# Copies of a block's masked factors issued from ScalarE's queue instead of SyncE's

## What is computed

```
xn = layernorm(x); sx = shifted(xn) - xn
x5 = xn + sx * (maa_stack + lora(xn, sx))              # five mixes: k, w, v, r, g
w  = exp(-exp(time_decay + lora(x5.w)))
r, k, v, g = x5.r @ Wr.T, x5.k @ Wk.T, x5.v @ Wv.T, silu(x5.g @ Wg.T)
for t in tokens:                                       # 32 heads of 16
    out[t] = r[t] @ (u * outer(k[t], v[t]) + s)
    s      = outer(k[t], v[t]) + w[t][:, None] * s
x = x + (groupnorm(out) * g) @ Wo.T
x = x + sigmoid(xr @ ffn_Wr.T) * (relu(xk @ ffn_Wk.T) ** 2 @ ffn_Wv.T)   # on layernorm(x)
```

## Time and profile before

| | us |
|---|---|
| median of 3 runs | 1509.73 |
| lowest and highest run | 1508.66, 1511.53 |
| the profiled execution, its own time | 1514.45 |
| span of the profiled execution, first to last instruction | 1512.7 |

### The profile page before, as it was taken

How to read it: one execution, slowest core, us unless ns; L and a number is a source line. 1 busy time by engine, 2 the same in 40 slices (tenths; PEclk the granted TensorE clock), 3 DMA queues, 4 the chain that set the end, 5 groups by cost and what they waited for, 6 DMA issues and landing times.

```text
span 1512.7 us, 52040 instructions
## 1 busy us (share of the span) xinstructions
PE 1443.9 (95%) x22980; PEld 1074.9 (71%) x22980; DVE 910.2 (60%) x1990; ACT 517.4 (34%) x910; POOL 599.2 (40%) x528
## 2 busy tenths in 40 slices
PE   8988999999999999999999999999999999999888
PEld 7867776757778676876767778576776757777464
DVE  3667557565676656657574676657657565665542
ACT  1323423424333333423433332333423424332332
POOL 3343515225262432615235262443615226262421
PEclk9999999999999999999999999999999999999899
DMA  8011102011010111102011110111102011010110
GB/s 309 6 42 49 42 12 69 18 40 54 28 55 15 41 54 37 55 12 70 18 41 54 28 55 14 41 55 38 55 19 63 18 40 54 14 55 15 56 33 28
DMA packets 56449, 68.13 MB, mean 45 GB/s; under 512 B 23264, under 2 KB 40032, under 8 KB 55200
## 3 DMA queue, kind: packets, MB, share of 16 engines
q1 hardware_dynamic: 56224, 64.79, 13.9%
HBM read 43.75 MB, written 8.39 MB: 34 GB/s over the span
## 4 chain that ended last, share of the span: by engine, by line
PE 84%; DVE 8%; SPq 3%; issue 2%; ACT 1%; DMA 1%; POOL 1%; DVEq 0%; ACTq 0%; POOLq 0%
PE pairs L1223 32%; PE pairs L1242 20%; PE at_ps L1151 4%; PE pairs L1234 4%; PE at_ps L1144 3%; SPq L406 3%; DVE x L778 3%; PE pairs L1250 3%; PE pairs L1266 3%; PE att_ps L1214 2%; PE pairs L1287 2%; PE pairs L1332 1%; PE pairs L1305 1%; PE pairs L1311 1%; PE pairs L1299 1%
## 5 line engine op out<-in xcount | busy, mean ns | idle before, releaser
L1223 PE MATMUL pairs<-x,wts 128*128 128x256 f32 x1760 | 397.0, 380 | 1.0 <-DVE lag L802 0.5
L1223 PEld LDWEIGHTS pairs<-x,wts 128*128 128x128 f32 x1760 | 328.4, 190 | 51.1 <-issue 7.0
L974 ACT ACTIVATE at<-at_ps 128x512 f32<-128x512 f32 x128 | 76.4, 597 | 386.1 <-PE at_ps L1151 193.5
L548 POOL TENSOR_TENSOR x<-x,xnT 128x1024 f32<-128x1024 f32 (+1 forms) x79 | 158.4, 2005 | 65.3 <-DVE x L778 65.3
L778 DVE SCALAR_TENSOR_TENSOR x<-pairs,vecs,sx 128x256 f32<-128x256 f32 x316 | 129.0, 474 | 87.0 <-PE pairs L1266 76.9
L558 POOL TENSOR_TENSOR bonv<-bonv,lag 128x256 f32<-128x256 f32 x32 | 27.1, 848 | 226.7 <-DVE lag L798 226.7
L1151 PE MATMUL at_ps<-rm,kc 128*16 128x128 f32 (+1 forms) x2048 | 112.8, 278 | 3.3 <-issue 3.3
L1223 PE MATMUL pairs<-yT,wts 128*128 128x256 f32 x512 | 113.8, 380 | 1.3 <-DVE gT L809 1.3
L1242 PE MATMUL pairs<-wts,cen 128*128 128x512 f32 x240 | 108.9, 606 | 4.5 <-DVE x L778 4.5
L1242 PE MATMUL pairs<-wts,yT 128*128 128x512 f32 x240 | 107.1, 599 | 1.6 <-POOL yT L585 1.6
L1223 PEld LDWEIGHTS pairs<-yT,wts 128*128 128x128 f32 x512 | 95.9, 190 | 14.2 <-DVE gT L809 1.5
(11 more groups left out here) (197 smaller groups left out, 2626.1 us busy)
## 6 DMA issues: line engine op xcount, KB each, us to landing
rm<-rst SPq DMA_DIRECT2D x1024, 12.0 KB
xu<-in_x SPq DMA_DIRECT2D x16, 512.0 KB, 3.9
wts<-in_wts SPq DMA_DIRECT2D x8, 1024.0 KB, 14.5
kvs<-in_s SPq DMA_DIRECT2D x32, 256.0 KB, 2.9
s<-in_s SPq DMA_DIRECT2D x32, 256.0 KB, 3.9
x<-in_x SPq DMA_DIRECT2D x15, 512.0 KB, 5.1
out<-sx SPq DMA_DIRECT2D x15, 512.0 KB, 3.0
prev<-in_prev SPq DMA_DIRECT2D x32, 4.0 KB, 3.8
```

The source lines that it names most:

```text
L548: gp.tensor_tensor(t, t, old, ALU.add).then_inc(x5_ready, 1)
L974: ac.activation(at[:, :, :], at_ps[:, :].rearrange("p (h t) -> p h t", h=HG), ACT.Copy)\
L1223: last = pe.matmul(ps[:, g // 2, TB * (g % 2):TB * (g % 2 + 1)], wts[:, m, k, g * P:(g + 1) * P], source[:, k, :], start=(k == 0), stop=(k ...
```

## The change

The copies of units 2 to 7 leave SP's list. `mask` on SP serves only units 0 and 1. On ACT, `evict` issues, directly behind its copy of unit n's products, the eight DMAs of unit n+2 within the same sequence; behind unit 3's copy it issues those of units 4 and 5, and behind those of units 2, 6 and 7 none. A new function `load_mask` does it; it waits for `rchain`, and the wait on `levels_done` is the one that `evict` has made already.

```diff
-SP_ORDER = ["x", "S0", "M1", "F1", "M2", "M3", "out", "x2", "S1", "M4", "M5", "F0", "M6", "M7", "M0"]
+SP_ORDER = ["x", "S0", "M1", "F1", "out", "x2", "S1", "F0", "M0"]
...
-    0: ["M1", "x", "F1", "M2", "M3", "out", "x2", "S1", "M4", "M5", "F0", "M6", "M7", "M0"],
-    LAST: ["S0", "M1", "F1", "x2@0", "x2@1", "M2", "M3", "M4", "out", "x2", "S1", "M5", "M6", "M7"],
+    0: ["M1", "x", "F1", "out", "x2", "S1", "F0", "M0"],
+    LAST: ["S0", "M1", "F1", "x2@0", "x2@1", "out", "x2", "S1"],
...
-                    elif name[0] == "M" and name != "M0" and units(i):
+                    elif name == "M1" and units(i):
                         mask(at_, int(name[1:]))
...
                 ac.activation(at[:, :, :], at_ps[:, :].rearrange("p (h t) -> p h t", h=HG), ACT.Copy)\
                   .then_inc(at_ready, 1)
+                for unit in {G - 2: (), G - 1: (G, G + 1), UNITS - 2: (), UNITS - 1: ()}.get(n, (n + 2,)):
+                    load_mask(at_, unit)
+
+            def load_mask(blk, n):
+
+                b, g, p = n // G, n % G, n % 2
+                ac.wait_ge(rchain, blk.count(2 * NR, NR * (b + 1)))
+                for h in range(HG):
+                    ac.dma_start(rm[p][S * h:S * (h + 1), h, :], rst[S * h:S * (h + 1), b, g, R16C:R64A])\
+                      .then_inc(rm_in[p], 16)
```

## The result

| | before | after |
|---|---|---|
| median, us | 1510.63 | 1783.67 |
| lowest and highest, us | 1508.66, 1513.22 | 1782.87, 1785.94 |
| ratio to before | | 1.181, interval 1.179 to 1.184 |
| span of the profiled execution, us | 1512.7 | 1782.2 |
| mean granted clock of PE | 0.991 | 0.914 |

The change costs 273 us; the prediction was 1778 us in 1685 to 1830. DVE's and POOL's lines are as before.

The account below looks back on a forecast made before the run. PE, busy 95% of the span, was taken to bound the kernel. Fifteen blocks at 14.2 us of stalls plus 3.4 of clock give 264, - 5 for the first blocks, + 10 for the last: 269, median 1778 us, range 1685 to 1830.

Parts of the forecast that it names:

- Price of a batch: ACT's list: eight copy issues hold it 5.65 us, sixteen 11.3, the same as on SP.
- Units 4 and 5, at kv1 and k.0: Behind E3, sixteen issues delay kt1 and z's tanh, so PE stalls at kv1 and k.0: 9.3 us.
- Unit 3, at hs_1: Behind E1, eight issues delay vtm1, so PE's hs_1 starts late: 4.9 us a middle block.
- Unit 2, at gn_sum: Behind E0, DVE's gn_sum starts 1.65 us late; 0.5 us is left over, inside the next stall: cost 0.
- a sign of being wrong: Prediction's test: wrong if a stall turns up at a place costed at nothing, such as gn_sum or r.
- Units 6 and 7: Behind E4 and E5: r's copy moves later, but g.0 needs its bank 3.4 us later still: cost 0.
- Clock: PE's clock falls once for each of two stalls, 1.7 us each, 3.4 us a block.
- yT: Last block, behind E3: sixteen issues make yT 10.3 us late, POOL's gate and wo follow: + 10.
- the clock holds: Rival: PE's clock doesn't fall, only the stalls cost, 15 x 14.2 = 213, + 5: 1728 us; chance 0.16.
- Queues hinder each other: Rival: ACT and SP take turns issuing, unit 2's batch takes 10 to 11 us: 1793 to 1838 us; chance 0.07.
- ACT issues as fast as the shortest row on SP: Rival: ACT's batch of eight takes 2.6 us, stalls of 5.1 us a block: 1605 us; chance 0.06.
- issues on ACT cost next to nothing: Rival: both stalls vanish below about 0.1 us an issue, leaving earlier copies: 1503 us, faster; chance 0.09.

Follow-up runs that it names:

- unit 2 alone: Against the kernel before, only unit 2's eight copies moved to ACT, behind E0; the other copies stay on SP: 1557.6 us, ratio 1.030.
- the second filling: Changed kernel plus dummy PE products: 6 ahead of vt_1, 6 ahead of hs_1, 34 ahead of kv1, 4 ahead of k.0: 1739.5 us, ratio 1.152.
- the fillings: Two kernels adding dummy PE products to the changed kernel where PE would stand idle, the second with more of them: 1756.1 and 1739.5 us.

## Why the prediction was right

The rows that it was built on were the right ones, and the largest terms came out as sized. By its steps, for a middle block:

- **Price of a batch**: 5.65 us forecast; 5.84 for eight and 11.00 for sixteen in the block shown, 6.60 for the eight of unit 2.
- **Units 4 and 5, at kv1 and k.0**: 9.3 forecast. From E3 to k.0 it is 13.33 us, before 4.33: 9.0.
- **Unit 3, at hs_1**: 4.9 forecast. From E1 to hs_1 it is 6.64 us, before 1.51: 5.1. Of PE's idle time there about half falls on vt_1 and half on hs_1, 3.22 and 2.06 us.
- **Unit 2, at gn_sum**: 0.5 us left over forecast, inside hs_1's stall. In the block shown it was 3.2, at vt_1, 2.3 on average, still inside that stall, so the sum didn't feel it. The size was wrong by two things: the batch took 6.60 us instead of 5.65, and DVE's L665 met POOL's L573. With unit 2 alone it showed as 3.0 us a block. By the prediction's own list a stall by way of gn_sum is a sign of being wrong: this step was, and the stall of unit 3 hid it.
- **Units 6 and 7**: 0 forecast, 0 measured in middle blocks.
- **Clock**: 3.4 forecast, 3.6 by the second filling and 4.4 by PE's busy time, with one fall for each stall as forecast.
- Together 17.6 forecast, 17.1 measured. Over the thirteen blocks 12.7 of it is idle time of PE and 4.4 slower work, where 14.2 and 3.4 were forecast; these two differences cancel in part.

Two terms at the edges were off and cancel. The fifteen blocks up to the last came to 248 us (13 x 17.07 + 11.0 + 15.2) where 264 - 5 = 259 were forecast, since each middle block gave 0.5 less (7 in all) and the first two together 9 less, where 5 were allowed for. From the last k.0 to the end it came to 21 where 10 were forecast: yT gave its 10, but the step failed that costed only yT there. It took unit 2's batch at nothing, as in a middle block, although the last block has a list of its own in which E1 stands behind gn_square (5.6), and it had no clock in that stretch, where PE's busy time grew from 145.3 to 153.2 us. So the median's closeness to 1778 owes something to luck; the middle block, 17.6 against 17.1, owes less.

Of the rivals, *the clock holds* would have been nearly right in the waits, and the fillings show how far: 1739 us with the clock kept up, where it had 1728. *Queues hinder each other* is refuted in its size: taking turns would have made unit 2's batch 10 to 11 us long, and it took 6.3 in the mean of blocks 1 to 14. The Trainium skill (Perfetto Trace Analysis, section DMA Instruction — HWDGE (DVE, Sync)) says that the block which makes descriptors is locked for exclusive use by the sequencer that uses it; no run here shows a wait for it, since SP's M1 took as long beside ACT's batch as without it, 6.33 and 6.30 us. *ACT issues as fast as the shortest row on SP* and *issues on ACT cost next to nothing* are refuted by the issue line itself, 514 ns at the shortest and 611 at the median.

## What to carry to other kernels

Each of these 12 KB copies took about 0.6 us of the list of the engine that issued it, on ACT as on SP, and a share of busy time doesn't show it. Before moving issues to an engine with idle time, look at what stands behind each place in its list and who waits for that: here the same 48 issues a block cost 17 us in one set of places and 0.3 in another. Read lists of first and last blocks separately, and add what the clock takes to each stall of PE, here about 2 us for each of the two.

## What the runs showed of the hardware that I had not expected

L665 on DVE takes 0.69 us in all 32 places before. In the changed kernel it takes 2.30 in eight places, in each of which POOL's L573 had started ahead of it, and there it ends 0.55 us behind the end of L573 each time; so it seems to have stood until POOL was done. In a ninth place L573 started 0.06 us behind it, and it took 0.69, as in the 23 others. The Trainium skill (SBUF — State Buffer, section Terms) says that DVE and GpSimd share a pair of ports under an exclusive lock held for a whole instruction, and that the loser is blocked; the trace agrees. In the block shown a shift of 1.5 us on DVE became one of 3.1 in this way.
